# Mamba's causal convolution as four shifted matmuls that accumulate in a PSUM bank, with a new plan

## The chip, the cores and the metric

The kernel runs on one core of one Trainium2 chip. The metric is the device time of one execution in microseconds, from the profiler's or the runtime's clock of the core; the median of the runs is the time of a kernel. All data are float32 unless said otherwise.

## The reference, cut to what matters

Sixteen sequences of 256 tokens with 128 features pass through two layers. Layer 0 adds a Mamba block and a mixture of eight experts, layer 1 adds an attention on spheres (16 heads) and a two-layer transformer with windowed attention. The change touches only the start of the Mamba block:

```python
x = L0_attn_x
xn = _layernorm(x, axis=-1)
x = x + mamba(xn) + experts(xn)
xn = _layernorm(x, axis=-1)
x = x + sphere_attention(xn) + windowed_transformer(xn)

def mamba(x):                                    # D_INNER 256, D_STATE 16, D_CONV 4
    xz = jnp.einsum('bld,ed->ble', x, in_proj_w)
    xc, z = jnp.split(xz, 2, axis=-1)
    xt = xc.transpose(0, 2, 1)
    xt = lax.conv_general_dilated(xt, conv_w, window_strides=(1,), padding=[(d_conv - 1, 0)],
                                  feature_group_count=d_inner, ...)
    xt = xt + conv_b[None, :, None]
    xs = jax.nn.silu(xt.transpose(0, 2, 1))
    ...                                          # x_proj, softplus, the scan over time, y * silu(z), out_proj
```

The convolution is causal and by channel: output channel e at time t is the sum over j = 0..3 of `conv_w[e, 3 - j] * xc[e, t - j]`. As xc is linear in x, tap j can be folded into the projection's weights and applied to the input shifted by j tokens.

## The kernel before

Two sequences form a pair of 512 tokens, and there are eight pairs (NPAIR). The work is cut into units, each of which passes through one or several engines in a row: `e_...` are the experts, `m_...` Mamba, `f_...` the layer norm between the layers, `g_...` the sphere attention, and the names in LAYER the windowed transformer. Mamba goes pair after pair. For a pair, `m_load` brings the transposed input xnTm (128 features by 512 tokens) into hB, four `m_in` units project it, `m_xp` and `m_dt` make the step sizes, `m_du` their products, and then 16 steps (STEPS) of `m_ex` (ScalarE exponentials, L1283), `m_bx` (VectorE product, L1484), `m_scan` (VectorE scan, L1490), `m_hc` (VectorE product, L1496) and `m_sum` (two identity matmuls that add up in a bank, L995) follow; `m_fin` and `m_out` (L1003) close the pair.

Of the four `m_in` units of a pair, k = 1 and 3 make z: one matmul of 128x128 weights with 512 columns (L975), then a SiLU on ScalarE straight from the bank (L1252). k = 0 and 2 make the two halves (c = 0, 1) of xs: one matmul of the same size, then on VectorE one tensor_scalar (L1460, last tap and bias) and three scalar_tensor_tensor (L1463, the other taps on 255, 254 and 253 tokens of each sequence), each waiting for the one before it, then a SiLU on ScalarE in place (L1255). There are 16 such units in all. `m_in` of a pair comes after `m_out` of the pair before.

The order of the units on every engine is static. `schedule()` simulates the engines when the kernel is built: among the units that are ready on an engine it takes the one with the smallest due time, `want`, which is a hand-set time plus a constant for the unit's kind (LATER) and one for its stream (STREAM), plus SWITCH where ScalarE would have to load another activation table. It takes the durations from `stages()` and the table STAGES, in microseconds. The names after the first in a unit's entry there are its engines in order; `m_in` for even k is `[("PE", 0.86), ("DVE", 3.15), ("ACT", 0.62)]`, `m_sum` is `[("PE", 1.72)]`, `m_bx` and `m_hc` `[("DVE", 1.22)]` each, `m_scan` `[("DVE", 2.28)]`. It also hands out the eight PSUM banks. Each engine then runs its list in order, with semaphore waits where data or a bank must be ready, so a unit that waits holds up everything behind it on its engine.

At the start, inputs and weights are loaded by DMAs issued from SyncE (`sync_setup`: the x tiles of the first two pairs, every second Mamba weight, the other x tiles, every second later weight) and from ScalarE (`scalar_setup`: the constants in `first`, the other Mamba weights, the other later weights, and only then the first activation table). `mamba_weights` (L890) negates exp(A_log) on VectorE once ScalarE has made it (L901), which waits for all Mamba weights (`d_wm`). The first `m_in` on TensorE waits for `d_wm` as well.

Of the kernel before, what the change touches and what calls it, by code (L numbers as in the profile page):

```python
# [10 lines left out]
P = 128  # L11
# [69 lines left out]
LOAD_TIME = 1.29  # L81

# [5 lines left out]
SWITCH = 103.0  # L88

LATER = {"down": -178, "e_down": 8, "e_lg": 188, "e_ln": 716, "e_load": -557, "e_place": -359, "e_pre": -546, "e_route": -350,  # L90
         "e_scat": -389, "e_store": -174, "e_tr": 351, "e_up": -1, "e_xn": -117, "e_xt": -22, "f_ln": 119, "f_tr": -365,
         "f_xn": 43, "f_yg": -410, "g_av": 42, "g_avT": -318, "g_ev": -787, "g_hd": -56, "g_ln": 110, "g_norm": -798, "g_oT":
         137, "g_out": 38, "g_pow": 138, "g_qkv": -40, "g_score": 2, "g_sq": -17, "g_sub": 6, "g_tan": -2, "gelu": -62,
         "heads": -11, "hid": -17, "l_weights": 328, "ln": -8, "ln2": 14, "lnT": 3, "m_B": -323, "m_C": -192, "m_bx": -26,
         "m_dt": 9, "m_du": -217, "m_ex": -27, "m_fin": 231, "m_hc": 9, "m_in": -14, "m_load": 506, "m_out": -1114, "m_scan":
         43, "m_sum": 4, "m_weights": -349, "m_xp": 474, "norm": 4, "oT": -14, "on": 0, "out": 21, "pt": -23, "pv": 57, "qkv":
         1, "qn": -18, "score": 10, "shift": 24, "up": -12, "wo": 56, "x_load": 594, "zeros": 223}

STREAM = {("e", 0): -23, ("e", 1): -94, ("e", 2): 9, ("e", 3): 106, ("e", 4): 299, ("e", 5): -2, ("e", 6): 65,
# [25 lines left out]
def stages(unit):  # L125
    u, n, b, k = unit
    if u == "m_in":
        return [("PE", 0.86), ("ACT", 0.62)] if k % 2 else [("PE", 0.86), ("DVE", 3.15), ("ACT", 0.62)]
    if u == "e_scat":
        return [("POOL", 1.5 * TT * (GP[n + 1] - GP[n]))]  # L130
    if u == "qkv":
        return [("PE", 0.86), ("ACT", 0.6)] if k % 3 else [("PE", 1.72), ("ACT", 1.02), ("DVE", 3.6), ("POOL", 2.36)]
    return STAGES[u]


def lands(unit, engine):
    return 2.0 if engine == "POOL" and unit[0] in ("e_scat", "f_yg") else LANDS[engine]

# [189 lines left out]
def takes_banks(unit):  # L328

    u, n, b, k = unit  # L330
    if u == "qkv" and k % 3 == 0:
        return (0, 2)
    if u in BANKS:
        return (1 if u == "g_hd" else 0, BANKS[u])
    if u == "e_pre" or (u == "e_lg" and n in GP) or (u == "m_sum" and k < CH) or (u == "g_av" and k % 2 == 0) or (u == "pv" and k % OH == 0):
        return (0, 1)
    return None
# [194 lines left out]
def build(nc, d, out):  # L532
    ctx = ExitStack()
    with ctx:
# [3 lines left out]
        def sem(name):  # L538
            return ctx.enter_context(nc.semaphore(name))
# [35 lines left out]
        w_in = load("in_projT", [P, 2 * DI], mamba)  # L575
        conv_w = load("conv_w", [P, CH, DC], mamba)
# [54 lines left out]

        gpad = sb("gpad", [P, HB, P])[:]
# [16 lines left out]
        arena = sb("arena", [P, 19168])  # L649
# [59 lines left out]
        ones_row = a0.get(NE)  # L709
# [21 lines left out]
        qks = a0.get(LAY, 2, 2, LD)  # L731
# [21 lines left out]
        p_in, v_conv, a_xs, a_zs, p_xp, a_dbl = sem("p_in"), sem("v_conv"), sem("a_xs"), sem("a_zs"), sem("p_xp"), sem("a_dbl")  # L753
# [134 lines left out]
        def mamba_weights():  # L888
            v.wait_ge(a_set, 1)
            v.tensor_scalar(a_neg[:], a_neg[:], -1.0, None, ALU.mult).then_inc(v_set, 1)  # L890
# [13 lines left out]
        def tensor_program():  # L904
            for u, i, b, k in order(plan, "PE"):
# [62 lines left out]
                elif u == "m_in":  # L968
                    z = k % 2
                    if i == 0:  # L970
                        t.wait_ge(d_wm, all_wm)
                    t.wait_ge(d_xm, 16 * (i + 1))
                    into(unit)
                    c = k // 2 + (2 if z else 0)
                    t.matmul(lb(), w_in[:, c * P:(c + 1) * P], xnTm, start=True, stop=True).then_inc(p_in, 1)  # L975
                    read_by(unit, a_zs if z else v_conv, CH * i + k // 2 + 1)
# [226 lines left out]
        def scalar_program():  # L1203
            for u, i, b, k in order(plan, "ACT"):
# [40 lines left out]
                elif u == "m_in":  # L1245
# [7 lines left out]
                    else:  # L1253
                        a.wait_ge(v_conv, CH * i + c + 1)
                        a.activation(xs[:, c], xs[:, c], ACT.Silu).then_inc(a_xs, 1)  # L1255
# [157 lines left out]
        def vector_program():  # L1413
            for u, i, b, k in order(plan, "DVE"):
# [39 lines left out]
                elif u == "m_in" and k % 2 == 0:  # L1454
                    c = k // 2
                    src, o = lb().rearrange("p (s l) -> p s l", s=2), xs[:, c].rearrange("p (s l) -> p s l", s=2)
                    v.wait_ge(p_in, 4 * i + k + 1)
                    if i:
                        v.wait_ge(p_mo, i)
                    v.tensor_scalar(o, src, conv_w[:, c, DC - 1:DC], conv_b[:, c:c + 1], ALU.mult, ALU.add).then_inc(v_own, nv.up())  # L1460
                    for j in range(1, DC):
                        v.wait_ge(v_own, nv.n)
                        e = v.scalar_tensor_tensor(o[:, :, j:], src[:, :, 0:L - j], conv_w[:, c, DC - 1 - j:DC - j], o[:, :, j:],  # L1463
                                                   ALU.mult, ALU.add)
                        if j < DC - 1:
                            e.then_inc(v_own, nv.up())
                        else:
                            e.then_inc(v_conv, 1)
# [398 lines left out]
def host_layout(a):  # L1867
# [5 lines left out]
    r["in_projT"] = f("L0_attn_in_proj_w").T  # L1873
    r["conv_w"] = halves(f("L0_attn_conv_w")[:, 0])
# [84 lines left out]
```

## Time and profile before

| | |
|---|---|
| median of 3 runs | 2333.68 us (2330.61 to 2341.05) |
| the profiled execution | 2321.25 us |
| its span, first to last instruction | 2320.0 us |
| TensorE matmul busy | 2018.4 us (87%) |
| TensorE weight load busy | 1379.7 us (59%) |
| VectorE busy | 1741.2 us (75%) |
| ScalarE busy | 1740.1 us (75%) |
| GpSimd busy | 613.1 us (26%) |
| mean granted TensorE clock | 0.904 of full speed |

PE is TensorE's matmul side, PEld its weight loads (they overlap matmuls), DVE VectorE, ACT ScalarE, POOL GpSimd, SP SyncE; a q behind a name is that engine's DMA-issuing or sequencing side. L975 is line 975 of the kernel. Every float32 matmul stands in the trace as two MATMUL records and two weight loads, so 32 matmuls are x64. A record of a matmul lasts longer than the distance to the next one, as they are pipelined; the distance between starts is what a row of matmuls costs. The profile is one execution; the median of the runs lies 12.4 us (0.5%) above it.

### The profile page before, as it was taken

How to read it: one execution, taken by the hardware profiler on the slowest of the kernel's cores; microseconds unless marked ns; L12 is line 12 of the kernel's file. 1: busy time of each engine (PE TensorE's matmuls, PEld its weight loads, DVE VectorE, ACT ScalarE, POOL GpSimd, SP SyncE). 2: the span in 40 equal slices, each digit the busy share in tenths (PEclk: the TensorE clock that was granted, in tenths of full speed). 3: DMA queues.
4: the chain of work that ended last, by engine and by line, in shares of the span. 5: the costliest groups of instructions: out<-in, count | busy, mean ns of one | idle time of the engine just before them, and what ended most of it. 6: DMA issues, size and time to landing. Idle time of an engine off the chain costs nothing.

```text
span 2320.0 us, 34433 instructions
## 1 busy us (share of the span) xinstructions
PE 2018.4 (87%) x12146; PEld 1379.7 (59%) x12146; DVE 1741.2 (75%) x2622; ACT 1740.1 (75%) x2948; POOL 613.1 (26%) x270
## 2 busy tenths in 40 slices
PE   3777888999889898999888897899998999899887
PEld 2544556786545565666555574566566665667566
DVE  5788896536898889868997688869997599864633
ACT  2435787888877689898787778768887788877982
POOL 2351222213222313322131312302233222222320
PEclk9788898999889898988999799899989899998889
DMA  6651114431120210011100111010100111000000
GB/s 225 210 178 56 55 46 142 128 116 59 39 64 19 70 55 33 10 38 51 47 26 7 51 56 46 10 47 29 59 28 10 43 51 64 1 1 3 4 1 6
DMA packets 67676, 126.57 MB, mean 55 GB/s; under 512 B 8852, under 2 KB 40276, under 8 KB 67380
## 3 DMA queue, kind: packets, MB, share of 16 engines
q1 hardware_dynamic: 61808, 113.19, 15.3%
q0 software_dynamic: 2816, 7.21, 0.9%
q10 hardware_dynamic: 2884, 3.96, 0.5%
q8 instruction: 101, 1.65, 0.3%
q14 instruction: 67, 0.55, 0.1%
HBM read 111.49 MB, written 12.85 MB: 54 GB/s over the span
## 4 chain that ended last, share of the span: by engine, by line
PE 62%; DVE 19%; issue 9%; ACT 6%; DMA 2%; SPq 2%; POOL 0%; DVEq 0%; ACTq 0%
PE ps L995 8%; PE ps L800 6%; PE ps L1097 5%; PE ps L1037 5%; PE ps L1130 3%; DVE hB L1490 3%; DVE hB L1496 3%; PE ps L1119 3%; PE ps L1137 3%; PE ps L1136 3%; PE ps L1051 2%; PE ps L1149 2%; PE ps L1151 2%; PE ps L1166 2%; PE ps L1150 2%
## 5 line engine op out<-in xcount | busy, mean ns | idle before, releaser
L1778 POOL TENSOR_TENSOR arena<-arena 128x1024 f32<-128x1024 f32 x128 | 355.0, 2796 | 869.0 <-ACT arena L1321 869.0
L1782 POOL TENSOR_TENSOR arena<-arena,rb 128x1024 f32<-128x1024 f32 x64 | 159.8, 2497 | 648.4 <-DVE rb L1620 648.4
L995 PE MATMUL ps<-hB,w_ident 128*128 128x512 f32 x512 | 281.8, 678 | 50.5 <-DVE hB L1496 50.5
L1490 DVE TENSOR_TENSOR_SCAN hB<-dA,hB 128x1024 f32<-128x1024 f32 x128 | 317.0, 2478 | 4.3 <-ACT dA L1283 4.1
L1484 DVE TENSOR_TENSOR hB<-BC,mv 128x1024 f32<-128x1024 f32 x128 | 196.1, 1536 | 41.6 <-PE ps L995 41.1
L800 PE MATMUL ps<-w_ident,arena 128*128 128x128 f32 x879 | 146.2, 315 | 70.0 <-DVE arena L1437 30.1
L1342 ACT ACTIVATE arena<-arena 128x256 f32<-128x256 f32 x512 | 205.4, 402 | 2.1
L1561 DVE TENSOR_SCALAR arena<-ps 128x1024 f32<-128x1024 f32 x128 | 154.9, 1217 | 68.9 <-PE ps L1037 68.5
L1283 ACT ACTIVATE dA<-mv,w_A_log 128x510 f32<-128x510 f32 x256 | 168.3, 712 | 45.9 <-DVE hB L1490 40.3
L1097 PE MATMUL ps<-w_l_wqkv,arena 128*128 128x512 f32 x384 | 190.9, 627 | 13.0 <-DVE rb L1620 4.1
L795 ACT ACT_TABLE_LOAD x139 | 178.3, 1283 | 19.2 <-issue 16.7
L995 PEld LDWEIGHTS ps<-hB,w_ident 128*128 128x128 f32 x512 | 98.4, 211 | 153.6 <-issue 91.5
L1496 DVE TENSOR_TENSOR hB<-hB,BC 128x1024 f32<-128x1024 f32 x128 | 188.7, 1476 | 0.3
L800 PEld LDWEIGHTS ps<-w_ident,arena 128*128 128x128 f32 x879 | 120.2, 163 | 103.6 <-issue 68.1
L1394 ACT ACTIVATE PT<-ps 128x640 f32<-128x640 f32 x128 | 89.3, 697 | 122.4 <-PE ps L1137 112.1
L1037 PE MATMUL ps<-gqT,gkT 8*128 8x256 f32 x1024 | 156.9, 466 | 24.3 <-DVE arena L1561 11.2
L1319 ACT ACTIVATE arena<-arena,one_b 128x2048 f32<-128x2048 f32 x64 | 128.0, 2000 | 36.5 <-DVE arena L1561 27.8
L1037 PEld LDWEIGHTS ps<-gqT,gkT 8*128 8x128 f32 x1024 | 95.9, 217 | 73.1 <-issue 62.6
L1137 PE MATMUL ps<-ident_q,nmx 128*128 128x192 f32 x512 | 131.6, 340 | 0.0
L1321 ACT ACTIVATE arena<-arena,one_b 128x2048 f32<-128x2048 f32 x64 | 128.2, 2003 | 2.1
L1337 ACT ACTIVATE arena<-arena,one_b 128x2048 f32<-128x2048 f32 x64 | 127.8, 1997 | 0.2
L1327 ACT ACTIVATE arena<-arena 128x2048 f32<-128x2048 f32 x64 | 121.9, 1905 | 2.5 <-POOL arena L1778 2.2
(219 smaller groups left out, 4406.8 us busy)
## 6 DMA issues: line engine op xcount, KB each, us to landing
BC<-bc_d SPq DMA_DIRECT2D x128, 512.0 KB, 3.7
BC<-in_experts SPq DMA_DIRECT2D x16, 514.0 KB, 3.3
arena<-in_experts SPq DMA_DIRECT2D x15, 514.0 KB, 4.3
mv<-in_experts SPq DMA_DIRECT2D x15, 514.0 KB, 3.3
arena<-in_x SPq DMA_DIRECT2D x8, 256.0 KB, 5.8
xnT_d<-arena SPq DMA_DIRECT2D x8, 256.0 KB, 2.6
hB<-xnT_d SPq DMA_DIRECT2D x8, 256.0 KB, 2.6
x<-in_x SPq DMA_DIRECT2D x8, 256.0 KB, 7.0
```

Of the source, the lines that this page charges most:

```text
L795: a.preload_act_table_set(names[0])
L800: return t.transpose(out_, in_, ident[0:k, 0:k])
L995: e = t.matmul(lb(), ident, hB[k % 2][:, j], start=q == 0 and j == 0, stop=q == NQ - 1 and j == NG - 1)
L1037: e = t.matmul(lb(z)[:, kt * L:(kt + 1) * L], gkT[32 * hi:32 * hi + GD, hb, kt * P:(kt + 1) * P], gqT[32 * hi:32 * hi + GD, hb], start=Tru ...
L1097: e = t.matmul(lb(z), hT1[b][:, tt * P:(tt + 1) * P], w_lqkv[:, l, (w + z) * INNER:(w + z + 1) * INNER], start=True, stop=True)
L1137: e = t.matmul(lb(z)[:, P:SC], top[1], ident_q[:], start=False, stop=True)
L1283: e = a.activation(dA[k % 2][:, j].rearrange("p (s l) -> p s l", s=2)[:, :, 1:], dtv[:, c].rearrange("p (s l) -> p s l", s=2)[:, :, 1:], A ...
L1342: e = a.activation(part, part, ACT.Exp, scale=-3.2, accum_out=vt[m % 2][:, kt, hi, GD + 2:GD + 3])
L1484: v.tensor_tensor(hB[k % 2], Bb[q % 2], bc(du[:, c:c + 1], [P, NG, T]), ALU.mult).then_inc(v_bx, 1)
L1490: v.tensor_tensor_scan(hf, flat2(dA[k % 2]), hf, 0.0, ALU.mult, ALU.add).then_inc(v_scan, 1)
L1496: v.tensor_tensor(hB[k % 2], hB[k % 2], Cb[q % 2], ALU.mult).then_inc(v_hc, 1)
L1778: g.tensor_tensor(la[m % 2][:, half], la[m % 2][:, half], cl[m % 2][:, half], ALU.subtract).then_inc(g_sub, 1)
```

## The change

- The two xs units of a pair no longer use VectorE. TensorE does four matmuls for each, of weights `w_conv[:, 3 - j]` (128x128) with the input shifted by j tokens within each sequence, all into one bank: 512, 510, 508 and 506 columns. ScalarE then applies SiLU with the bias `conv_b` from the bank.
- The weights are made on the chip: the taps are loaded replicated over the partitions (`conv_rows`, 128x4x256, 512 KB), the projection's x half (`in_xT`, 128 KB) into a part of gkT that is free at the start, and `mamba_weights` multiplies them on VectorE in one instruction of 128x1024 elements. The z half of the projection is a tile of its own (128 KB). Before, the projection was one load of 256 KB and the taps one of 4 KB.
- The first `m_in` waits for that product (`v_set` 3) instead of the loads.
- To make room the arena shrinks by 528 columns: qk_scale lies in gqT at first, ones_row in PT.
- The wait for `m_out` of the pair before moves from VectorE to ScalarE.
- Planning: `m_in` for even k is `[("PE", 3.42), ("ACT", 0.7)]`; all PE durations are divided by CLOCK = 0.88; SWITCH goes from 103 to 181; all of LATER and STREAM are new; `g_av` takes its bank at its second stage (PE) and not at its first (DVE).

The diff, without the numbers of LATER and STREAM:

```diff
+CLOCK = 0.88
...
-SWITCH = 103.0
+SWITCH = 181.0
...
-def stages(unit):
+def durations(unit):
     u, n, b, k = unit
     if u == "m_in":
-        return [("PE", 0.86), ("ACT", 0.62)] if k % 2 else [("PE", 0.86), ("DVE", 3.15), ("ACT", 0.62)]
+        return [("PE", 0.86), ("ACT", 0.62)] if k % 2 else [("PE", 3.42), ("ACT", 0.7)]
...
+def stages(unit):
+    return [(e, time / CLOCK if e == "PE" else time) for e, time in durations(unit)]
...
+    if u == "g_av" and k % 2 == 0:
+        return (1, 1)
-    if u == "e_pre" or (u == "e_lg" and n in GP) or (u == "m_sum" and k < CH) or (u == "g_av" and k % 2 == 0) or (u == "pv" and k % OH == 0):
+    if u == "e_pre" or (u == "e_lg" and n in GP) or (u == "m_sum" and k < CH) or (u == "pv" and k % OH == 0):
         return (0, 1)
...
-        w_in = load("in_projT", [P, 2 * DI], mamba)
-        conv_w = load("conv_w", [P, CH, DC], mamba)
+        w_z = load("in_zT", [P, DI], mamba)
+        w_conv = load("conv_rows", [P, DC, DI], mamba)
...
+        w_x = flat2(gkT)[:, 0:DI]
+        mamba.append((w_x, d["in_xT"]))
...
-        arena = sb("arena", [P, 19168])
+        arena = sb("arena", [P, 18640])
...
         def mamba_weights():
             v.wait_ge(a_set, 1)
+            v.wait_ge(d_wm, all_wm)
+            v.tensor_tensor(w_conv[:], w_conv[:], bc(w_x.unsqueeze(1), [P, DC, DI]), ALU.mult)
             v.tensor_scalar(a_neg[:], a_neg[:], -1.0, None, ALU.mult).then_inc(v_set, 1)
...
                     if i == 0:
-                        t.wait_ge(d_wm, all_wm)
+                        t.wait_ge(v_set, 3)
...
-                    c = k // 2 + (2 if z else 0)
-                    t.matmul(lb(), w_in[:, c * P:(c + 1) * P], xnTm, start=True, stop=True).then_inc(p_in, 1)
-                    read_by(unit, a_zs if z else v_conv, CH * i + k // 2 + 1)
+                    mine = slice(k // 2 * P, (k // 2 + 1) * P)
+                    if z:
+                        e = t.matmul(lb(), w_z[:, mine], xnTm, start=True, stop=True)
+                    else:
+                        src, o = (x_.rearrange("p (s l) -> p s l", s=2) for x_ in (xnTm, lb()))
+                        for j in range(DC):
+                            e = t.matmul(o[:, :, j:], w_conv[:, DC - 1 - j, mine], src[:, :, 0:L - j], start=j == 0, stop=j == DC - 1)
+                    e.then_inc(p_in, 1)
+                    read_by(unit, a_zs if z else a_xs, CH * i + k // 2 + 1)
...
-                        a.wait_ge(v_conv, CH * i + c + 1)
-                        a.activation(xs[:, c], xs[:, c], ACT.Silu).then_inc(a_xs, 1)
+                        a.wait_ge(p_in, 4 * i + k + 1)
+                        if i:
+                            a.wait_ge(p_mo, i)
+                        a.activation(xs[:, c], lb(), ACT.Silu, bias=conv_b[:, c:c + 1]).then_inc(a_xs, 1)
...
-                elif u == "m_in" and k % 2 == 0:
-                    ...
-                    v.tensor_scalar(o, src, conv_w[:, c, DC - 1:DC], conv_b[:, c:c + 1], ALU.mult, ALU.add).then_inc(v_own, nv.up())
-                    for j in range(1, DC):
-                        v.wait_ge(v_own, nv.n)
-                        e = v.scalar_tensor_tensor(o[:, :, j:], src[:, :, 0:L - j], conv_w[:, c, DC - 1 - j:DC - j], o[:, :, j:],
-                                                   ALU.mult, ALU.add)
```

## Rows read from the trace of the kernel before

**Rows 1.** The page: busy us of each engine, and the mean granted clock.

```profile
PE 2018.4 (87%) x12146; PEld 1379.7 (59%) x12146; DVE 1741.2 (75%) x2622; ACT 1740.1 (75%) x2948; POOL 613.1 (26%) x270
core 0: 2320.0 us, clock 0.904
```

**Rows 2.** The page, shares of the span in the chain that ended last.

```profile
PE 62%; DVE 19%; issue 9%; ACT 6%; DMA 2%; SPq 2%; POOL 0%; DVEq 0%; ACTq 0%
```

**Rows 3.** Stretches: PE, PEld, DVE, ACT, POOL busy us (instructions), PE clock, DMA share, GB/s.

```profile
0.00:60.00 60.00, 21.80 (x77) 13.35 (x78) 30.47 (x142) 14.70 (x33) 14.40 (x22) 0.92 0.67 224
...
400.00:600.00 200.00, 187.83 (x1385) 146.89 (x1384) 99.97 (x201) 171.70 (x351) 46.28 (x22) 0.97 0.32 97
...
1400.00:1600.00 200.00, 169.02 (x1030) 111.56 (x1030) 165.28 (x234) 154.10 (x248) 57.78 (x24) 0.92 0.10 31
...
200.00:2000.00 1800.00, 1613.23 (x9782) 1093.86 (x9784) 1439.71 (x2014) 1438.83 (x2404) 471.80 (x185) 0.91 0.16 50
```

**Rows 4.** Waits of PE: us in total, how many, the longest.

```profile
PE ps L995 <- DVE hB L1496: 50.5, 33, 4.9
PE ps L1051 <- DVE vt L1573: 33.0, 8, 8.3
...
PE ps L800 <- DVE gpad L1553: 14.6, 6, 7.0
```

**Rows 5.** The same in three of the eight stretches that hold a pair's m_in.

```profile
35.00:55.00 20.00, 11.16 (x34) 5.39 (x34) 15.60 (x61) 7.29 (x16) 6.78 (x7) 0.83 0.19 59
...
1518.00:1553.00 35.00, 34.59 (x214) 23.50 (x212) 26.36 (x63) 26.02 (x52) 2.37 (x1) 1.00 0.00 1
1763.00:1790.00 27.00, 27.00 (x163) 17.67 (x159) 21.95 (x41) 24.45 (x42) 2.36 (x1) 1.00 0.01 2
```

**Rows 6.** The timeline of TensorE at the first pair's m_in: start us, us, what.

```profile
37.27 3.42 PE L975 MATMUL ps<-hB,w_in_projT 128*128 128x512 f32 x4 [2.88 <-DMA hB<-xnT_d]
...
41.09 0.19 PEld L975 LDWEIGHTS ps<-hB,w_in_projT 128*128 128x128 f32 x1 [0.24 <-issue]
...
41.52 0.19 PEld L975 LDWEIGHTS ps<-hB,w_in_projT 128*128 128x128 f32 x1 [0.24 <-issue]
```

**Rows 7.** Groups by line: count, busy us, mean ns, idle before.

```profile
L995 PE MATMUL ps<-hB,w_ident 128*128 128x512 f32 x512 | 281.8, 678 | 50.5 <-DVE hB L1496 50.5
L1484 DVE TENSOR_TENSOR hB<-BC,mv 128x1024 f32<-128x1024 f32 x128 | 196.1, 1536 | 41.6 <-PE ps L995 41.1
L1463 DVE SCALAR_TENSOR_TENSOR mv<-ps,w_conv_w,mv 128x510 f32<-128x510 f32 (+2 forms) x48 | 35.8, 746 | 1.7
L1173 PE MATMUL ps<-xd,w_ident 128*128 128x128 f32 x64 | 13.1, 288 | 0.0
L1003 PE MATMUL ps<-w_out_projT,mv 128*128 128x128 f32 x128 | 17.6, 296 | 6.4 <-DVE mv L1502 6.4
L1460 DVE TENSOR_SCALAR mv<-ps,w_conv_w,w_conv_b 128x512 f32<-128x512 f32 x16 | 12.8, 802 | 4.9 <-PE ps L975 4.9
```

**Rows 8.** The timeline of the first 40 us.

```profile
6.36 0.45 ACTq L853 DMA_DIRECT2D w_conv_w<-in_conv_w  x1
...
12.87 1.45 SPq L847 DMA_DIRECT2D w_l_wo<-in_l_wo  x1
...
16.70 1.28 ACT L795 ACT_TABLE_LOAD   x1 [16.70 <-issue]
...
18.56 2.14 DVE L1437 TENSOR_SCALAR arena<-arena 128x128 f32<-128x128 f32 x8 [3.43 <-ACT arena L1220]
...
29.67 0.88 DVE L1429 BATCH_NORM_STATS2 arena<-arena 128x6 f32<-128x128 f32 x4 [8.97 <-DMA arena<-in_x]
...
30.88 0.15 DVE L890 TENSOR_SCALAR w_A_log<-w_A_log 128x32 f32<-128x32 f32 x1
```

**Rows 9.** The SiLU from the bank (L1252) and the one in place (L1255): ns min/median/max.

```profile
L1252 ACT ACTIVATE mv<-ps x16: 579/594/647, 45.5 to 1806.3; 128x512 f32<-128x512 f32 x16
...
L1255 ACT ACTIVATE mv<-mv x16: 629/630/638, 44.9 to 1804.9; 128x512 f32<-128x512 f32 x16
```

More of the change, by code:

```diff
@@ L87 @@
          "norm": "ln", "pt": "ln", "ln": "ln", "m_in": "silu", "g_tan": "tan", "gelu": "gelu"}
-SWITCH = 103.0
[L90 to L99, printed above, removed]
[13 rows of a table removed]
+SWITCH = 181.0
+LATER = {"down": -245, "e_down": -30, "e_lg": -7, "e_ln": 598, "e_load": -976, "e_place": -8, "e_pre": -880, "e_route": -475,
+         "e_scat": 581, "e_store": -867, "e_tr": 450, "e_up": -22, "e_xn": -354, "e_xt": -508, "f_ln": 444, "f_tr": -1292,
+         "f_xn": 607, "f_yg": 51, "g_av": 76, "g_avT": -1499, "g_ev": -1486, "g_hd": -37, "g_ln": 491, "g_norm": -371, "g_oT":
+         485, "g_out": 56, "g_pow": 502, "g_qkv": 455, "g_score": 13, "g_sq": 43, "g_sub": 1014, "g_tan": 31, "gelu": -532,
+         "heads": -25, "hid": -23, "l_weights": -51, "ln": 9, "ln2": 66, "lnT": 1, "m_B": -422, "m_C": -429, "m_bx": -26,
+         "m_dt": 1, "m_du": -691, "m_ex": 27, "m_fin": 422, "m_hc": 89, "m_in": -66, "m_load": 207, "m_out": -1109, "m_scan":
+         835, "m_sum": 5, "m_weights": -569, "m_xp": 1741, "norm": -227, "oT": -43, "on": -186, "out": 66, "pt": -4, "pv": 75,
+         "qkv": 12, "qn": 26, "score": -11, "shift": 58, "up": -224, "wo": 78, "x_load": 427, "zeros": 571}
+STREAM = {("e", 0): 107, ("e", 1): -197, ("e", 2): 125, ("e", 3): 188, ("e", 4): 556, ("e", 5): 4, ("e", 6): 86,
[13 rows of a table added]
 LOADED = [15.0, 24.0]
@@ L708, in build @@
         gate, rank = a0.get(NE), a0.get(NE)
-        ones_row = a0.get(NE)
+        ones_row = PT[0][:, 1, 0:NE]
         before_b, ones_b = a0.get(P, dt=BF16), a0.get(P, dt=BF16)
@@ L730, in build @@
         mask, maskT = PT[0][:, 0], PT[1][:, 0]
-        qks = a0.get(LAY, 2, 2, LD)
+        qks = flat2(gqT)[:, 0:LAY * 4 * LD].rearrange("p (l k w e) -> p l k w e", l=LAY, k=2, w=2)
         first += [(w_before, d["before"]), (gate, d["gateT"]), (rank, d["rank"]), (mask, d["mask"]), (maskT, d["maskT"])]
@@ L752, in build @@
         d_xm, d_x1, d_bc, d_B, d_C = sem("d_xm"), sem2("d_x1"), sem("d_bc"), sem2("d_B"), sem2("d_C")
-        p_in, v_conv, a_xs, a_zs, p_xp, a_dbl = sem("p_in"), sem("v_conv"), sem("a_xs"), sem("a_zs"), sem("p_xp"), sem("a_dbl")
+        p_in, a_xs, a_zs, p_xp, a_dbl = sem("p_in"), sem("a_xs"), sem("a_zs"), sem("p_xp"), sem("a_dbl")
         a_abs, v_du = sem("a_abs"), sem("v_du")
@@ L1452, in vector_program @@
                     v.tensor_tensor(ye[q][made_in(i)], lb()[:, 0:DM], b2E[q][weights_in(i)[0]], ALU.add).then_inc(v_y, 1)
-                elif u == "m_in" and k % 2 == 0:
[L1455 to L1459, printed above, removed]
-                    v.tensor_scalar(o, src, conv_w[:, c, DC - 1:DC], conv_b[:, c:c + 1], ALU.mult, ALU.add).then_inc(v_own, nv.up())
-                    for j in range(1, DC):
-                        v.wait_ge(v_own, nv.n)
-                        e = v.scalar_tensor_tensor(o[:, :, j:], src[:, :, 0:L - j], conv_w[:, c, DC - 1 - j:DC - j], o[:, :, j:],
-                                                   ALU.mult, ALU.add)
[L1465 to L1468, printed above, removed]
                 elif u == "m_du":
@@ L1872, in host_layout @@
     r["x"] = f("L0_attn_x").reshape(NPAIR, T, DM)
-    r["in_projT"] = f("L0_attn_in_proj_w").T
-    r["conv_w"] = halves(f("L0_attn_conv_w")[:, 0])
+    r["in_xT"], r["in_zT"] = f("L0_attn_in_proj_w").T[:, 0:DI], f("L0_attn_in_proj_w").T[:, DI:]
+    r["conv_rows"] = rep(f("L0_attn_conv_w")[:, 0].T)
     r["conv_b"] = halves(f("L0_attn_conv_b"))
```

26 rows, old and new, of the table STREAM are left out of this document.

## Prediction

> **What bounds the kernel now.** I read the page's busy times first [rows 1]. TensorE's matmuls are busy for 2018.4 us of 2320.0, VectorE and ScalarE for 1741.2 and 1740.1. So TensorE is idle for 302 us in all. The table of stretches says where [rows 3]: 38 us of it lie in the first 60 us, when data is still coming, and 187 us between 200 and 2000 us, where TensorE is busy for 1613.2 of 1800 us, 89.6%. The best stretch of 200 us there reaches 187.8 us (94%), at a granted clock of 0.97; one that holds little but steady state, 1400 to 1600, reaches 169.0 us (84.5%). Then the waits [rows 4]: the largest on TensorE's side are on VectorE, 50.5 us for the last product of a Mamba step, 33.0 us in eight waits for the small vt product of the sphere attention, 14.6 us for gpad. ACT and DMA account for much less. The chain that ended last goes through TensorE for 62% of the span and VectorE for 19% [rows 2]. TensorE is the bound; what it loses, it loses mostly to VectorE's being late.
>
> **The matmuls that are added.** Each of the 16 xs units gets three more matmuls of 510, 508 and 506 columns, 48 in all. Two records make a matmul, and at the high clock the records start 0.43 us apart (weight loads at 41.09 and 41.52, each 0.19 us long and hidden in that distance) [rows 6], so one costs 0.86 us and 48 cost 41 us. At the low clock two matmuls took 3.42 us, 1.71 each [rows 6], so 82 us is the upper bound. I stay near the lower: the stretches that hold `m_in` ran at a granted clock of 1.00 in the two later rows [rows 5]; the first pair alone was partly at the low one; its six matmuls cost up to 0.85 us more each, 5 us. I take +46 us of TensorE. The moving operand becomes two pieces with a gap and the output too. No matmul of 510 columns has that shape here; the nearest is the layer norm's 128-column one with a strided input and output, 288 ns against 296 ns for the plain one of `m_out` [rows 7], so I put nothing on it.
>
> How much of it lies on the path? In the two later stretches TensorE is 99 and 100% busy [rows 5]: it did not stand idle while VectorE convolved, it did other units' work. So nothing there hides the 46 us; they push everything that is behind. Only the first pair's stretch has room (11.2 of 20 us busy) [rows 5], which hides its 10 us. I count +38 us.
>
> **What VectorE loses.** 12.8 + 35.8 = 48.6 us go [rows 7], and the product of the weights comes in, 128x1024 elements, at most the 1.54 us of `m_bx`, which has this size [rows 7]. That is 47 us or 2.7% of its work. Its worth on the path: 19% of the span is 441 us out of 1741 us of VectorE's work on the chain [rows 1, 2], one in four, so 12 us. Bounds are 0 (the waits stay where they are, because they belong to the Mamba step's own chain of product, scan and product) and -47 (TensorE waits for VectorE for longer than that, so all of it could come back). I take -12. ScalarE's 16 SiLUs from the bank cost 594 ns instead of 630 [rows 9]: -0.6 us, nothing. The chain of a unit hardly moves, 0.86 + 3.0 + 0.63 us before, 3.4 + 0.6 after, and a bank is held for about 4 us either way. The new wait for `m_out` on ScalarE costs nothing, since TensorE's own order puts `m_in` behind it.
>
> **The start.** ScalarE's queue issues the taps' load, now 512 KB instead of 4 KB, and one load more. The small one took 0.45 us to issue, one of 512 KB 1.45 [rows 8], so the queue is 1.0 + 0.45 = 1.5 us later with its first table load, for which VectorE waits at 18.56 [rows 8]. The other end is the traffic: 512 KB more at the 224 GB/s of the first 60 us [rows 3] is 2.3 us, ahead of the x tiles for which VectorE waits 8.97 us [rows 8]. TensorE stands idle there, so this is on the path: +3 us (0 to +5). The product of the weights sits in VectorE's order where `L890` was, at 30.88 us, over six us ahead of the first `m_in` at 37.27 [rows 6, 8]; what is queued behind it, the routing, is 1.5 us later at worst, within the same +5. With the order as it was, the sum is 38 - 12 + 3 = +29 us.
>
> **The new order.** This is the largest unknown, and no row shows it. The old plan priced TensorE at its full speed: `m_sum` at 1.72 us, where the trace has 281.8 / 128 = 2.20 us [rows 7]; with 0.88 it is 1.95. The mean granted clock of 0.904 [rows 1] is close to the new figure. An order made with TensorE too fast puts matmuls on its list before their inputs are there, and lets VectorE's small urgent operations come too late: the 33.0 us for vt in eight waits of up to 8.3 us, for an operation of 0.3 us, are of this kind, and the 14.6 us for gpad too [rows 4]. I take it that the new order removes as much as these two, 47 us, of the 264 us that TensorE idles after the first 60. The bounds: it removes nothing or adds 20 (below), or it brings the whole middle to the 94% of the best stretch [rows 3], (1613 + 38) / 0.94 = 1756 us instead of 1800 + 29, about -73.
>
> **Sum.** +29 - 47 = -18 us, on the profiled execution's 2321.25 us (a span of 2320.0 and 1.25 around it) 2303 us; the median of the runs shown is 12.4 us higher than that execution, which gives 2316 us against 2333.68.
>
> **A word on the clock.** TensorE is granted 0.904 of full speed [rows 1]; with two levels, 1.2 and 2.4 GHz, about 19% of the span, 445 us, was at the low one, and at the rows' 1.71 against 0.86 us per matmul the work done there could have taken half, up to 220 us less [rows 6]. The level was low where TensorE had stood idle (0.83 in the first pair's stretch at 56% busy, 1.00 at 99 and 100%) [rows 5]. The Trainium skill says as much (TensorE: Matmul & The Clock Gate, Part 1: the default state is throttled, and activity releases it), and these rows agree. By that rule the added matmuls, which come as dense groups, may pay for part of themselves.
>
> **Rivals.** (a) The order gets dense and the clock follows. If TensorE waits 73 us less instead of 47, and a fifth of the 445 us at the low level turns high, 89 us in which the work is done in half, of which I count half as it overlaps with the first, another -22: 29 - 73 - 22 = -66, 2268 us. For it: stretches at 94 to 100% busy at 0.97 to 1.00 exist [rows 3, 5]. Against it: 1763 to 1790 is one stretch; the middle as a whole is at 0.91 [rows 3]. (b) The order gives back just what the matmuls cost, 29 us: 2334 us, no change. For it: the moves are between two engines that both stand near full in the steady state (VectorE 165 of 200 us in 1400 to 1600) [rows 3]. (c) Slower: the moved work is paid in full on TensorE and the order doesn't help. The mechanism is in the Mamba step: the plan prices its three VectorE operations at 1.22 + 2.28 + 1.22 = 4.72 us, the trace has 1.54 us for the first alone [rows 7]. With TensorE now priced nearly right and VectorE still too cheap, the plan believes that VectorE is ahead, gives `m_sum` its place too early, and TensorE waits for the product L1496 more than the 50.5 us of now [rows 4]. It decides as soon as less than 29 us of TensorE's idle time is won back. With nothing won it is +29, 2363 us; if the waits on L1496 grow by 40%, +20 more, 2383 us. (d) The change does not do what it says, for example if the shifted matmuls run at twice the price: another +41 us on (b) or (c), over 2375. Only the shape speaks for it, and the 128-column row against it.
>
> **Chances.** The forecast, 2300 to 2325 us, 0.36; (a), 2255 to 2300, 0.15; (b), 2325 to 2345, 0.20; (c), 2345 to 2385, 0.26; (d) 0.03. About 0.5% (12 us) is what a measurement of this kernel can tell from no change. Faster by more than that, below 2322: nine tenths of the forecast and all of (a), 0.48. Slower by more, above 2345.4: (c) and (d), 0.29. Within: 0.23. The range from 2264 to 2374 leaves out the lower fifth of (a) and the upper end of (c) with (d), about 0.14 in all. The outcomes have both signs; the forecast's own range is 2300 to 2325.
>
> **What would show it.** Right: the matmuls of `m_in` are 160 records with starts 0.43 us apart; VectorE busy about 1694 us; TensorE busy near 2060 us, in which its rise is 40 to 50 us less what the clock gives; the wait of L1051 on L1573 small; TensorE's idle time near 240 us. The first matmul of the experts one to three us later than 19.8. Wrong: TensorE idle still 300 us or more (then c), its busy time up by 80 (then d), the granted clock at 0.93 or above (then a), or the waits on L1496 grown.

## The result, and the profile after

The changed kernel takes 2362.84 us (median of 4 runs, 2347.68 to 2366.09), the kernel before 2332.14 us on the same chip (4 runs, 2329.35 to 2341.05). The ratio is 1.0112, 95% interval 1.0060 to 1.0164: slower by 26 us, with an interval of 14 to 38. The forecast was 2316 us and faster; the sign is wrong, though the time lies inside the stated range (2264 to 2374).

The page of the changed kernel: span, busy times, and the cores' line, against [rows 1].

```profile
span 2364.8 us, 34581 instructions
PE 2072.3 (88%) x12242; PEld 1412.8 (60%) x12242; DVE 1706.5 (72%) x2559; ACT 1764.9 (75%) x2965; POOL 597.1 (25%) x270
core 0: 2364.8 us, clock 0.898
```

The 96 records of the 48 matmuls are there (12242 - 12146). TensorE's busy time rose by 53.9 us, its idle time fell from 301.6 to 292.5. VectorE lost 34.7 us, where I had 47, and ScalarE gained 24.8. The chain that ended last, against [rows 2], and the table loads, then those of the kernel before:

```profile
PE 51%; DVE 20%; issue 13%; ACT 9%; SPq 3%; DMA 2%; POOL 1%; DVEq 0%; ACTq 0%; POOLq 0%
L805 ACT ACT_TABLE_LOAD x156 | 200.1, 1283 | 17.7 <-issue 15.0
```

```profile
L795 ACT ACT_TABLE_LOAD x139 | 178.3, 1283 | 19.2 <-issue 16.7
```

The kernel before had 139 loads. The new order has 17 more, although its SWITCH is larger, and they are 21.8 us of ScalarE's 24.8. By stretch, against [rows 3]; the columns are the same:

```profile
0.00:60.00 60.00, 23.81 (x88) 15.07 (x89) 26.35 (x136) 16.90 (x34) 14.43 (x22) 0.99 0.67 230
...
400.00:600.00 200.00, 186.71 (x1278) 141.37 (x1276) 98.14 (x182) 157.52 (x333) 35.92 (x18) 0.94 0.36 107
...
1400.00:1600.00 200.00, 187.81 (x1151) 125.61 (x1150) 164.61 (x241) 152.21 (x254) 51.83 (x21) 0.96 0.11 37
...
200.00:2000.00 1800.00, 1637.18 (x9731) 1104.83 (x9730) 1415.44 (x1959) 1425.39 (x2367) 458.19 (x184) 0.91 0.16 50
```

The middle is denser than before (91.0% against 89.6%), and 1400 to 1600 rose from 169.0 to 187.8 us. Yet by 2000 us only 10241 of 12242 records are through, 2004 are left (three are counted on both sides), where before there were 1878. What remains takes 364.8 us at 84% busy, where before it took 320.0 at 88%; the granted clock is 0.88 in this stretch, where it was 0.92. First the changed kernel, then the one before:

```profile
2000.00:2430.00 430.00, 308.11 (x2004) 226.82 (x2001) 166.25 (x344) 265.90 (x429) 76.71 (x32) 0.88 0.01 2
```

```profile
2000.00:2430.00 430.00, 281.25 (x1878) 205.56 (x1870) 163.78 (x331) 228.88 (x376) 73.12 (x30) 0.92 0.01 2
```

Waits of TensorE in the changed kernel, against [rows 4] (L810 is L800 of before, L1013 L995, L1069 L1051, L1055 L1037, L1184 L1166, L1206 L1188, L1132 L1114):

```profile
PE ps L1013 <- DVE hB L1501: 26.3, 19, 4.0
...
PE ps L810 <- DVE arena L1635: 20.2, 8, 5.4
...
PE ps L1184 <- ACT arena L1417: 11.5, 6, 4.0
PE ps L810 <- DVE arena L1678: 11.5, 5, 5.4
PE ps L1055 <- DVE rb L1625: 11.3, 8, 4.4
PE ps L810 <- DVE gpad L1558: 10.7, 5, 3.4
PE ps L1206 <- DVE arena L1683: 10.7, 8, 3.2
PE ps L1132 <- ACT arena L1406: 9.9, 7, 4.9
PE ps L1069 <- DVE vt L1578: 8.9, 5, 4.0
```

The waits that I had named did shrink: 50.5 to 26.3, 33.0 to 8.9, 14.6 to 10.7, 52 us together. But six others of this list, which the reader sees here, stood before at 9.6, 3.9, 3.6, 4.3, 1.6 and 5.4 us and stand now at 20.2, 11.5, 11.5, 11.3, 10.7 and 9.9: 47 us more. The rows that show the same for the kernel before are these:

```profile
PE ps L800 <- DVE arena L1630: 9.6, 8, 2.3
...
PE ps L1114 <- ACT arena L1386: 5.4, 3, 3.3
...
PE ps L1037 <- DVE rb L1620: 4.3, 5, 1.5
...
PE ps L1166 <- ACT arena L1397: 3.9, 4, 1.8
...
PE ps L800 <- DVE arena L1673: 3.6, 3, 2.3
...
PE ps L1188 <- DVE arena L1678: 1.6, 3, 0.8
```

These are picked rows; all of TensorE's idle time together fell by 9 us.

The matmuls themselves, and the instruction that makes the weights:

```profile
L992 PE MATMUL ps<-hB,w_conv_rows 128*128 128x512 f32 (+3 forms) x128 | 61.2, 622 | 1.5 <-DMA hB<-xnT_d 0.8 <-ACT arena L1392 0.7
L901 DVE TENSOR_TENSOR w_conv_rows<-w_conv_rows,gkT 128x1024 f32<-128x1024 f32 x1 | 1.2, 1192 | 0.0
```

```profile
1499.61 3.58 PE L992 MATMUL ps<-hB,w_conv_rows 128*128 128x512 f32 x8
```

Eight records in 3.58 us, 0.43 us apart, as the plain ones of [rows 6], and 622 ns long on average, as the 621 ns of the unshifted ones in e2 below: the shifted operand in two pieces costs nothing extra.

### The profile page after: what moved, and what is told of

It is laid out like the page before. It is cut to its first block, busy times and chain, and to the rows that moved or that the text cites. A ratio compares the mean times of both kernels' runs of the same rounds, so it can differ in the third digit from the quotient of the medians.

```text
span 2364.8 us, 34581 instructions
## 1 busy us (share of the span) xinstructions
PE 2072.3 (88%) x12242; PEld 1412.8 (60%) x12242; DVE 1706.5 (72%) x2559; ACT 1764.9 (75%) x2965; POOL 597.1 (25%) x270
## 4 chain that ended last, share of the span: by engine, by line
PE 51%; DVE 20%; issue 13%; ACT 9%; SPq 3%; DMA 2%; POOL 1%; DVEq 0%; ACTq 0%; POOLq 0%
PE ps L1013 6%; PE ps L810 5%; PE ps L1115 4%; PE ps L1055 4%; DVE hB L1495 3%; PE ps L1148 3%; DVE hB L1489 3%; PE ps L1155 2%; PE ps L1154 2%; PE ps L1137 2%; PE ps L1167 2%; PE ps L1184 2%; PE ps L1069 2%; PE ps L1169 2%; DVE hB L1501 2%
## 5 line engine op out<-in xcount | busy, mean ns | idle before, releaser
L1783 POOL TENSOR_TENSOR arena<-arena 128x1024 f32<-128x1024 f32 x128 | 346.3, 2727 | 781.6 <-ACT arena L1341 781.6
L1013 PE MATMUL ps<-hB,w_ident 128*128 128x512 f32 x512 | 277.4, 670 | 27.5 <-DVE hB L1501 26.3
L810 PE MATMUL ps<-w_ident,arena 128*128 128x128 f32 x879 | 150.2, 320 | 110.9 <-DVE arena L1457 32.1
L810 PEld LDWEIGHTS ps<-w_ident,arena 128*128 128x128 f32 x879 | 121.4, 165 | 144.8 <-issue 94.1
L1055 PE MATMUL ps<-gqT,gkT 8*128 8x256 f32 x1024 | 160.2, 465 | 32.2 <-DVE arena L1566 13.1
L1013 PEld LDWEIGHTS ps<-hB,w_ident 128*128 128x128 f32 x512 | 97.4, 208 | 126.9 <-issue 89.4
L1501 DVE TENSOR_TENSOR hB<-hB,BC 128x1024 f32<-128x1024 f32 x128 | 172.7, 1352 | 0.6
L1055 PEld LDWEIGHTS ps<-gqT,gkT 8*128 8x128 f32 x1024 | 98.2, 216 | 78.7 <-issue 65.8
L1167 PEld LDWEIGHTS ps<-arena,PT 128*128 128x128 f32 x512 | 88.3, 203 | 59.7 <-issue 46.1
```

The lines of the kernel that those rows point to most:

```text
L810: return t.transpose(out_, in_, ident[0:k, 0:k])
L1013: e = t.matmul(lb(), ident, hB[k % 2][:, j], start=q == 0 and j == 0, stop=q == NQ - 1 and j == NG - 1)
L1055: e = t.matmul(lb(z)[:, kt * L:(kt + 1) * L], gkT[32 * hi:32 * hi + GD, hb, kt * P:(kt + 1) * P], gqT[32 * hi:32 * hi + GD, hb], start=Tru ...
L1501: v.tensor_tensor(hB[k % 2], hB[k % 2], Cb[q % 2], ALU.mult).then_inc(v_hc, 1)
L1783: g.tensor_tensor(la[m % 2][:, half], la[m % 2][:, half], cl[m % 2][:, half], ALU.subtract).then_inc(g_sub, 1)
```

## The experiments

My theory, A, was now: the matmuls cost what the sum said (+29 us with the rest of the move), and the new order gives back little. The rival, B: the move is near neutral and the new order itself is slower. All ratios are to the kernel before on the same chip, whose medians were 2335.48, 2335.11 and 2335.81 us in the three groups of four; one percent is 23.4 us.

### The move on the old order

```diff
 # e1: the changed kernel's body; schedule() is the old one with the old constants, then
+    for z, x in [y for y in zip(starts["DVE"], plan["DVE"]) if y[1][0] == "m_in"]:
+        at = plan["ACT"].index(x)
+        del plan["ACT"][at], starts["ACT"][at]
+        at = sum(1 for y in starts["ACT"] if y < z)
+        plan["ACT"].insert(at, x)
...
+    plan["DVE"] = [x for x in plan["DVE"] if x[0] != "m_in"]
```

> The changed convolution (four matmuls, weights made on the chip, no VectorE part) on the order of the kernel before: every list is the old plan's, VectorE's part is struck from its list and ScalarE's SiLU stands where VectorE's first tap stood, since it now frees the bank. Theory A (the work moved onto TensorE costs what my sum said, and the new order is worth little): +29 us on before, about 2361. Rival B (the move costs nothing on the old order and the new order is what lost the time): 2325 to 2340. In the new place the SiLUs need more table loads, which can add up to 15 us of ScalarE's time; that would be seen in its busy time.

Measured: 2348.19 us, ratio 1.0046 (1.0013 to 1.0079), +11 us, of 10 runs. It carries 153 table loads. Theory A's +29 is outside, and the time is 8 us above the range of B.

### The matmuls alone, and the taps alone

```diff
 # e2, in the kernel before
-                    t.matmul(lb(), w_in[:, c * P:(c + 1) * P], xnTm, start=True, stop=True).then_inc(p_in, 1)
+                    for j in range(1 if z else DC):
+                        e = t.matmul(lb(), w_in[:, c * P:(c + 1) * P], xnTm, start=True, stop=True)
+                    e.then_inc(p_in, 1)
 # e3, in the kernel before
-                    for j in range(1, DC):
...
-                        e = v.scalar_tensor_tensor(o[:, :, j:], src[:, :, 0:L - j], conv_w[:, c, DC - 1 - j:DC - j], o[:, :, j:],
-                                                   ALU.mult, ALU.add)
```

> The kernel before, each of the 16 xs units issuing its matmul four times into the same bank (each overwrites the one before), all else and the order as before: only the 48 matmuls are added. Theory A: TensorE is full in these stretches, so +38 us, 2370, with TensorE busy 41 to 46 us more. Rival B: TensorE's later idle time takes it up, +0 to +10 us.

Measured: 2359.38 us, ratio 1.0104 (1.0073 to 1.0136), +24 us. Its group of matmuls, then the page's busy line and the cores' line:

```profile
L976 PE MATMUL ps<-hB,w_in_projT 128*128 128x512 f32 x160 | 76.2, 621 | 6.1 <-DMA hB<-xnT_d 3.6 <-DVE mv L1465 2.5
```

```profile
PE 2046.6 (88%) x12242; PEld 1393.5 (60%) x12242; DVE 1740.0 (74%) x2622; ACT 1740.6 (74%) x2948; POOL 613.0 (26%) x270
core 0: 2338.5 us, clock 0.909
```

The group had 34.5 us in the kernel before, for 64 records; it is 42 us dearer now, between the 41 and the 46 us that I had. The whole engine is busy only 28 us more, at a granted clock of 0.909 against 0.904, and its idle time is 10 us less (291.9 us). The time, 2359, lies between the two expectations.

> The kernel before without the three scalar_tensor_tensor of each xs unit (48 operations, 35.8 us of VectorE), which are left out of the computation; all else and the order as before. Theory A: one in four of VectorE's microseconds is on the path, -9 us, 2323. Rival: VectorE's convolution was covered by TensorE's other work altogether, 0. Third case: the whole comes back, -36 us, 2296.

Measured: 2318.52 us, ratio 0.9896 (0.9824 to 0.9969), -24 us by the ratio, -17 by the medians; its interval reaches from -41 to -7. By the middle value half or more of VectorE's 35.8 us comes back, but Theory A's quarter, -9 us, lies inside the interval, and so does the whole.

### The new order alone

```diff
 # e4: the kernel before; schedule(), CLOCK, stages() and the constants are the changed kernel's, then
+    for x in [y for y in plan["PE"] if y[0] == "m_in" and y[3] % 2 == 0]:
+        at = sum(1 for z in starts["DVE"] if z < ends["PE", x])
+        plan["DVE"].insert(at, x)
...
```

> The kernel before with its own convolution on VectorE, on the order of the changed kernel: its plan is taken literally, and VectorE's part of a unit is put into VectorE's list at the planned time at which TensorE's part ends. Theory A: the new order is worth what the result leaves after +29, close to 0: 2325 to 2340. Rival B: the new order is itself the loss (17 more table loads, a tail that is 45 us longer): 2355 to 2370. My forecast had it at -47: 2286.

Measured: 2370.83 us, ratio 1.0136 (1.0109 to 1.0163), +32 us. The same instructions as in the kernel before (x12146 and x2622), but for 17 table loads:

```profile
PE 2049.2 (86%) x12146; PEld 1405.0 (59%) x12146; DVE 1753.1 (74%) x2622; ACT 1762.5 (74%) x2965; POOL 599.4 (25%) x270
core 0: 2370.8 us, clock 0.889
```

TensorE idles 321.6 us instead of 301.6. Its waits show the same new ones as the changed kernel has:

```profile
PE ps L814 <- DVE arena L1644: 27.4, 9, 6.3
PE ps L1009 <- DVE hB L1510: 25.7, 20, 4.0
...
PE ps L1051 <- DVE rb L1634: 15.2, 8, 4.7
...
PE ps L1180 <- ACT arena L1411: 10.9, 6, 4.0
```

So with the old convolution the order alone makes the loss, and more: on it the changed convolution is 0.24% faster than the old one (1.0112 against 1.0136), about 6 us, with intervals that overlap. With the changed convolution the order is worth less: from e1 to the changed kernel it is +26 - 11 = +15 us (by the two intervals some 1 to 29, on two chips). A falls. Of B, the part on the order stands; its other part, a move that costs nothing, holds only roughly (e1). e4 has a limit: its lists were planned without the 3 us that VectorE spends on each unit there, so a part of the 32 can be that mismatch.

### Why the new order is slower: table loads?

```diff
 # e5, in the kernel before, at g_tan
                     use(SIG, GELU, SILU)
+                    if m % 4 == 1 or m == 2:
+                        a.preload_act_table_set(table[0])
```

> The kernel before with 17 more activation-table loads on ScalarE, each loading the table that is already there, right before a tanh of the sphere attention; order and work as before. The new order has just 17 loads more than the old one (156 against 139). Theory C (ScalarE's extra loads are what makes the new order slow): 17 x 1.28 = 22 us of ScalarE, nearly all on the path, +15 to +25 us, 2355. Rival D (the loads are covered, and the new order loses by TensorE's waits and by its clock): +0 to +7 us.

Measured: 2339.62 us, ratio 1.0025 (0.9994 to 1.0056), +6 us (-1 to +13). The trace shows 16 loads more, not the 17 that I meant:

```profile
L1327 ACT ACT_TABLE_LOAD x16 | 20.5, 1283 | 0.3
```

Twenty microseconds of ScalarE cost about six. Loads at other places may cost otherwise, but they do not explain 32.

```diff
 # e6: e1, but 11 of the 16 SiLUs stay at their old place in ScalarE's list
+        if 2 * x[1] + x[3] // 2 in [0, 1, 2, 3, 5, 6, 7, 8, 9, 12, 13]:
+            continue
```

> The changed convolution on the old order, as in e1, but 11 of the 16 SiLUs stand at their old place in ScalarE's list instead of at VectorE's first tap; 146 table loads instead of 153. Theory C: 7 loads fewer are -6 to -9 us on e1, about 2341 against e1's 2348. Rival D: as e1 within 3 us.

Measured: 2385.89 us, ratio 1.0203 (1.0166 to 1.0240), +47 us, 38 us slower than e1 with seven loads fewer. Neither theory had this. The old place is later than VectorE's first tap, and in this kernel ScalarE is who frees the bank. Who waited for that SiLU (L1280) in e6:

```profile
  PEld ps L815: 12.0, 4
  PE ps L815: 11.2, 4
  PE ps L1120: 3.3, 1
  PEld ps L1220: 2.4, 1
  PE ps L1004: 2.1, 1
  PE ps L1220: 1.5, 1
```

In e1 TensorE waits 0.8 us in all for the SiLU. The matmuls' waits sum to 18 us here. I did not single out the other 20 us; e6 ran at a median granted clock of 0.8945 and e1 at 0.907, which by the slope worked out at the end (some 20 us for 0.01) is about 25 of the 38 us. The two accounts overlap, and neither was tested apart.

```diff
 # e9: e1's body on the old order in all lists; VectorE empties the bank, the SiLU stays in place
+                elif u == "m_in" and k % 2 == 0:
...
+                    v.tensor_scalar(xs[:, k // 2], lb(), conv_b[:, k // 2:k // 2 + 1], None, ALU.add).then_inc(v_conv, 1)
```

> The changed convolution on the order of the kernel before, in all lists: four matmuls on TensorE, then VectorE empties the bank with one operation that adds the bias (0.8 us instead of 3.0), then the SiLU in place at its old place in ScalarE's list; 139 table loads. If e2 (+24) and e3 (-17 to -24 for 36 us of VectorE) add up, this is 2335 to 2345. If what made e6 slow was the bank that ScalarE freed late and not the four matmuls, this is back near e1 or below, 2335 to 2350; if the late SiLU itself was it, it is near e6, above 2370.

Measured: 2349.45 us, ratio 1.0067 (1.0040 to 1.0095), +16 us. With the SiLUs at the same late place as in e6 but the bank freed early, the 32 us between them are gone (the median clock is 0.9045 against 0.8945, so part of them came by way of the clock). So it is the bank that ScalarE frees late, not the SiLU's lateness.

### Why it is slower: the clock factor, the constants, or any plan?

```diff
 # e7, in the changed kernel: SWITCH = 103.0, LATER and STREAM of the kernel before
 # e8, in the kernel before
+CLOCK = 0.88
...
-def stages(unit):
+def durations(unit):
...
+def stages(unit):
+    return [(e, time / CLOCK if e == "PE" else time) for e, time in durations(unit)]
 # e11, in the kernel before
-        return [("PE", 0.86), ("ACT", 0.62)] if k % 2 else [("PE", 0.86), ("DVE", 3.15), ("ACT", 0.62)]
+        return [("PE", 0.86), ("ACT", 0.62)] if k % 2 else [("PE", 0.86), ("DVE", 3.05), ("ACT", 0.62)]
 # e12, in the kernel before
-SWITCH = 103.0
+SWITCH = 106.0
```

> The changed kernel whole, with CLOCK = 0.88, but SWITCH, LATER and STREAM of the kernel before: planned anew with constants that belong to another set of durations. It has 143 table loads. If the due times of the change are bad in themselves, this is better than the changed kernel: 2330 to 2350. If any plan that is not searched for its own durations comes out worse, and the new constants are about as good as one gets, it is at 2365 or above.

Measured: 2397.64 us, ratio 1.0245 (1.0200 to 1.0290), +57 us.

> The kernel before, with only the planner's TensorE durations divided by 0.88; its constants, convolution and computation stay. It has 150 or more table loads instead of 139. My prediction's step (a plan that prices TensorE rightly loses less to waits): at or below before, 2300 to 2335. Rival (constants and durations belong together, and right prices help only with a search): 2345 to 2380.

Measured: 2381.15 us, ratio 1.0204 (1.0166 to 1.0243), +48 us.

> The kernel before with one number of the planner changed: VectorE's part of the xs unit is priced 3.05 instead of 3.15 us, which is nearer the trace's 3.04. The computation is the same; the lists come out in another order (144 table loads). If the constants are tuned to their exact durations, so that any other plan is worse: 2355 to 2390, as e8. If the plan is robust and e8 lost by the clock factor itself: 2325 to 2345.

Measured: 2418.85 us, ratio 1.0341 (1.0296 to 1.0385), +80 us, for one price moved by 0.1 us towards what the trace has, and more than the 2390 that was expected at most. Its page and its largest wait:

```profile
PE 2080.1 (86%) x12146; PEld 1415.5 (58%) x12146; DVE 1737.2 (72%) x2622; ACT 1749.2 (72%) x2953; POOL 593.8 (24%) x270
core 0: 2427.2 us, clock 0.881
```

```profile
PE ps L995 <- DVE hB L1496: 71.0, 34, 6.2
```

> The kernel before with SWITCH at 106 instead of 103, all else the same; 143 table loads. As e11: 2350 to 2390 if any plan other than the searched one is worse, 2325 to 2345 if the plan is robust.

Measured: 2367.54 us, ratio 1.0119 (1.0075 to 1.0163), +28 us.

Four plans whose constants were not made for their durations lie 28, 48, 57 and 80 us above the kernel before, and none is near it. The changed kernel's own order, at +32, is at the good end of that spread. So the constants of the change did repair something: e7, the same durations with the old constants, is at +57, the change at +26. They only didn't reach the order of before.

### What the matmuls cost on the new order

```diff
 # e10, in the changed kernel
-                        for j in range(DC):
+                        for j in range(1):
...
```

> The changed kernel without the three shifted matmuls of each xs unit (they are left out of the computation), order and all else as in the changed kernel. My step (nothing hides the matmuls): -38 us on the changed kernel's 2363, 2325. By e2's measure, -24, 2339. If the new order, which was planned with them, hides them: -10 or less, 2353 or above. In no case is it far below the kernel before, since the order costs what e4 shows.

Measured: 2359.88 us, ratio 1.0096 (1.0063 to 1.0129), +22 us, against +26 with the matmuls: 4 us, where the same work costs 24 on the old order, and the intervals leave room for some 20. That the new order hides nearly all of them is not shown. The two profiles are at nearly one clock (0.896 and 0.898), and there the matmuls cost 16 us: TensorE is busy 37 us more and idle 21 us less (292.5 against 313.5).

```profile
PE 2035.2 (87%) x12146; PEld 1397.2 (59%) x12146; DVE 1711.6 (73%) x2559; ACT 1764.2 (75%) x2965; POOL 598.0 (25%) x270
core 0: 2348.7 us, clock 0.896
```

The rest of the difference goes with the clock: the median is 0.891 in e10 and 0.900 in the changed kernel.

## Why the prediction was wrong, point by point

**The bound and the places of idle time** were read rightly, and the counts came out: 160 records, 0.43 us apart, one product of the weights, of 1.19 us, where I had bounded it by 1.54. TensorE's busy time came to 2072 us against my 2060, its idle time to 292.5 against my 240.

**The matmuls: +46 us of TensorE, +38 on the path.** e2 gives +42 us in their own group and +24 (17 to 32) in time. The price held; the share on the path was 14 us too large on the old order, and on the new one it was some 4 us by the medians (e10). (My sum had a slip too: 46 less the 10 that the first pair hides is 36.) "Nothing there hides the 46 us" was wrong in part: idle time took up 10 us in e2's profile and 21 in e10's. The larger part of what was missing is the clock. e2 ran at a median of 0.9005 against 0.895, an estimated 11 us given back; at the clock of before it would be +35.

**VectorE: 12 us for 47.** e3 gives 24 us (7 to 41) for 36. Whether the chain's share of VectorE, one in four, was too low a price is not settled: e3's median clock was 0.8995, by which an estimated 9 of the 24 us came, and the interval holds the 9 that the share gives. Both terms together are +24 - 24 = 0, where I had +26; at equal clocks they are an estimated +35 - 15 = +20. VectorE's busy time fell by 48.5 us on the old order (to 1692.7 in e1), about as forecast; on the new one 12 us of that are missing, for a reason given at the end. The SiLU from the bank with its bias took 688 ns (median), not 594: 16 of them are 0.9 us more, not 0.6 less.

**The start: +3.** The x tiles of [rows 8] landed 3.0 us later in the changed kernel:

```profile
32.68 0.87 DVE L1449 BATCH_NORM_STATS2 arena<-arena 128x6 f32<-128x128 f32 x4 [13.66 <-DMA arena<-in_x]
```

The issue queue is not what did it; the first table load came at 15.02 us, sooner than at 16.70, and the load of the taps took 0.45 us to issue as before. That leaves the traffic, the other end of the bound, which no run tested by itself. One profile can't tell 3 us here: the same instruction started at 30.77 in e1 and 31.48 in e9, and between 28.69 (e2) and 30.43 (e4) with the old loads. The experts' first matmul came at 18.14 us, sooner than the 19.82 of before, not later as I had said. The sum of the parts measured on the old order, 24 - 24 + 3, is +3 where e1 has +11 (3 to 18) and e9 +16; e1's 14 more table loads may be 5 of it. The rest stays open.

**The clock, at nothing in the sum.** I had written that the added matmuls may pay for part of themselves, and gave that no term. At equal clocks the work terms come to about +35 - 15 + 3 = +23 by e2 and e3, and e1 itself to +35, around my +29; by time e1 is +11. The 24 us between are the estimate at the end for its clock of 0.907.

**The new order: -47.** This is the step that failed, and it made the sign. It measured +32 with the old convolution (e4) and +15 with the changed one (e1 to the changed kernel), a loss both times. I had taken waits that looked like faults of order, and assumed that an order made with the right TensorE price would remove them and put nothing in their place. It did remove them, 52 us; six others grew by 47, and in e4 all of TensorE's idle time grew by 20. The belief behind it, that a plan with truer prices is a better plan, is refuted twice without the convolution: e8 has the truer TensorE prices and is 48 us slower, e11 has a truer price of one unit and is 80 us slower. That the order of before is fast because its constants were picked for exactly its durations fits all four replans, but how they were picked is in no run, and none made a new set; why one plan waits more than another is open too. The lower bound of this term, "removes nothing or adds 20", holds the +15, was too tight by 12 us for e4, and by 60 for the worst replan. It should have been centred at a loss.

**The rivals.** The time is that of (c), 2363, by luck and not by its mechanism: the waits on the last product of the Mamba step fell from 50.5 to 26.3 us instead of growing by 40%. Its reading of a row was wrong too. The 1.54 us for `m_bx` is a mean that 28 long ones of 128 raise; the median is 1.22 us, just what the plan has. The plan has the usual length right and lacks the long ones, which the last section explains. (b), no change, is out by the interval of 14 to 38 us. (d) is out by the 0.43 us. But for (c)'s 20 us on L1496, which did not come, none of them had an order that is worse by itself.

**A slip of basis.** The profiled execution of before was a quick one, 2321.25 us at a granted clock of 0.904; the median of before is at 0.894 to 0.895 in the three groups. Across the 13 runs of before in the first group (0.889 to 0.905) a run is 20 us shorter for each 0.01 of clock (24 and 20 in the other two groups). A difference of two profiles at different clocks, such as the +31 us in TensorE's busy time of e4 at 0.889, mixes the kernel with its run. By medians e4 is at 0.8905, 0.0045 below, which by that slope is 9 of its 32 us; some 23 are left for the order. No version that computes the whole result is faster than the kernel before; e3, the only faster one, leaves out the taps.

## What to carry to other kernels

A static order that came out of tuned constants can be a part of the kernel with a value of its own: four other plans cost 28 to 80 us of 2335, two of them from prices made truer. So price a change of work and a change of order apart, put a loss into the middle of the range for a new order, and test the work on the old order with its lists kept as they are. When an evacuation moves to another engine, ask at what place in that engine's list it stands: the bank is free only then (e6 against e9, 32 us).

## What the runs showed of the hardware that I had not expected

**The clock followed TensorE's idle time.** The kernel before runs at a median granted clock of 0.895. With the 48 matmuls added to the same order it is 0.9005 (e2), without the taps and with no matmul added 0.8995 (e3), and with the whole move 0.907 (e1) and 0.9045 (e9), each the median of 4 to 10 runs. Over all kernels here, those whose profile has TensorE idle for less than 295 us (e1, e2, e3, e9, the changed one) have a median clock of 0.8995 or more, and those with more than 300 us (all others) 0.8975 or less, down to 0.886 at 347 us in e11. It agrees with the rule of the Trainium skill (TensorE: Matmul & The Clock Gate, Part 1) that activity releases the throttle, which I had written down and given no term. By the slope of 20 us per 0.01, measured between runs of one kernel and so an estimate here, e1 got 24 us back that way, and its +11 would be +35 without it. The changed kernel's median is 0.900. If its own kernel before, whose clocks are not on record, stood at the 0.895 of the other groups, its +26 would be +36 at that clock, about e1's +35: what the new order cost the changed convolution would then have come mostly by way of the clock. Which of the two, idle time or clock, moved the other is not separated by any run.

**The slow ones among VectorE's products lie beside one of GpSimd's.** The product L1496 took 1476 ns on average before and 1352 as L1501 after, the product L1630 1230 before and 1460 as L1635 after.

```profile
L1501 DVE TENSOR_TENSOR hB<-hB,BC 128x1024 f32<-128x1024 f32 x128 | 172.7, 1352 | 0.6
L1635 DVE TENSOR_TENSOR arena<-arena,lss 128x1024 f32<-128x1024 f32 x64 | 91.7, 1460 | 3.6 <-ACT lss L1399 3.6
```

The instructions are the same, and so is their usual time. Minimum, median and maximum in ns, first before and then after, and the longest one of before with what GpSimd did at that time:

```profile
L1496 DVE TENSOR_TENSOR hB<-hB,BC x128: 1191/1215/7217, 78.1 to 2004.0; 128x1024 f32<-128x1024 f32 x128
L1501 DVE TENSOR_TENSOR hB<-hB,BC x128: 1193/1218/3432, 87.6 to 1979.0; 128x1024 f32<-128x1024 f32 x128
```

```profile
1218.31 7.22 DVE L1496 TENSOR_TENSOR hB<-hB,BC 128x1024 f32<-128x1024 f32 x1
1217.47 6.96 POOL L1778 TENSOR_TENSOR arena<-arena 128x1024 f32<-128x1024 f32 x3
```

The means move by a few long ones. Of the 128 L1496 before, 20 took over 1.3 us, of the 128 L1484 28, of the 64 L1630 one; after, the same lines have 13, 26 and 10. Every one of these overlaps a tensor_tensor of GpSimd in the trace, of the short ones one in ten or fewer. Over all of VectorE, instructions that took at least 0.9 us more than their line's median, all beside a GpSimd tensor_tensor, add up to 131 us above it before, 129 in e1, 143 in the changed kernel and 145 in e4. So the new order puts some 12 us more of VectorE's work beside GpSimd's, and that is what its busy time lacks of the 47. GpSimd's spans are rough, and no run moved its work, so what a plan without these meetings would give is open.
